# Expert feed-forward stage of a graph layer: node tiles in groups of four instead of two

## What is computed

```python
def _L0_ffn_ref(x, Wr, br, W1, b1, g1, be1, m1, v1, W2, b2, g2, be2, m2, v2, Wo, bo):
    feat = jnp.mean(x, axis=0)
    w = jax.nn.softmax(feat @ Wr + br, axis=-1)
    h = jnp.einsum('bfd,edh->bfeh', x, W1) + b1
    h = jax.nn.relu(_bn(h, g1, be1, m1, v1))
    h = jnp.einsum('bfeh,ehk->bfek', h, W2) + b2
    h = jax.nn.relu(_bn(h, g2, be2, m2, v2))
    y = jnp.einsum('bfeh,ehd->bfed', h, Wo) + bo
    return jnp.einsum('bfed,fe->bfd', y, w)
...
x = x + _L0_ffn_ref(_layernorm(x, axis=-1)[None], ...)[0]
```

## Time and profile before

| | |
|---|---|
| runs | 2795.51, 2791.87, 2793.63 us; median 2793.63 |
| span of the profiled execution | 2870.7 us |
| PE busy in it | 2525.6 us, 88% |
| DVE, ACT, POOL busy | 2235.1, 1570.5, 930.4 us |
| chain that ended last, by engine | PE 67%, DVE 19%, issue 7% |
| chain that ended last, L1378 and L1388 | 20% and 10% |

### The profile page before, as it was taken

One profiled execution on the slowest core, in us unless ns is written; L12 is line 12 of the kernel. 1 busy time (PEld: TensorE's weight loads), 2 busy tenths in 40 slices (PEclk: granted clock), 3 DMA queues, 4 the chain that ended last, 5 costly groups with the idle time before them and its releaser, 6 DMA issues.

```text
span 2870.7 us, 48875 instructions
## 1 busy us (share of the span) xinstructions
PE 2525.6 (88%) x15682; PEld 2185.1 (76%) x15682; DVE 2235.1 (78%) x4426; ACT 1570.5 (55%) x3233; POOL 930.4 (32%) x891
## 2 busy tenths in 40 slices
PE   6379995788988889988888989858999999999999
PEld 4266773567767767767767767648999999999999
DVE  6796553698998899899898899857777777777775
ACT  5422110355555656556555555546666666666665
POOL 0140003456666666656666666600000000000000
PEclk9798997799999999999999999978999999999999
DMA  5031445566666666666666666630000000000000
GB/s 157 22 108 43 139 137 178 147 192 190 194 195 192 193 196 194 189 193 192 198 197 190 189 194 194 189 100 12 16 16 16 12 14 14 16 16 16 16 14 10
DMA packets 190069, 336.68 MB, mean 117 GB/s; under 512 B 31472, under 2 KB 129040, under 8 KB 189798
## 3 DMA queue, kind: packets, MB, share of 16 engines
q0 software_dynamic: 67104, 219.09, 25.4%
q1 hardware_dynamic: 122726, 114.53, 13.2%
HBM read 293.83 MB, written 40.48 MB: 116 GB/s over the span
## 4 chain that ended last, share of the span: by engine, by line
PE 67%; DVE 19%; issue 7%; another core or an unknown queue 2%; ACT 1%; DMA 1%; DVEq 1%; SPq 0%; POOL 0%; ACTq 0%; POOLq 0%
PE ps L1378 20%; PE ps L1274 10%; PE ps L1388 10%; PE ps L1263 7%; PE ps L1140 4%; DVE ring L1726 3%; PE ps L1241 3%; PE ps L1234 3%; DVE ring L1779 2%; DVE rows L1478 2%; PE ps L1219 1%; PE ps L1056 1%; DVE nodes L1793 1%; PE ps L1063 1%
## 5 line engine op out<-in xcount | busy, mean ns | idle before, releaser
L798 POOL DMA_INDIRECT ring<-kv_rows,idx x832 | 877.2, 1054 | 796.5 <-DMA idx<-src_cols 276.3
L1378 PE MATMUL ps<-f_split,e_up 128*128 128x256 f32 (+1 forms) x3200 | 595.4, 287 | 5.0 <-DVE e_low L1938 5.0
L980 ACT ACTIVATE f_more<-ps,e_rest 128x256 f32<-128x256 f32 (+1 forms) x800 | 401.9, 552 | 259.5 <-PE ps L1378 257.4
L1378 PEld LDWEIGHTS ps<-f_split,e_up 128*128 128x128 f32 x3200 | 501.0, 193 | 9.3 <-DVE e_low L1938 5.7
L1263 PE MATMUL ps<-nodes,ohT 128*128 x1664 | 418.1, 396 | 89.2 <-issue 62.6
L1274 PE MATMUL ps<-ring 128*128 128x260 f32 x1664 | 454.5, 420 | 0.0
L1378 PE MATMUL ps<-f_split,e_low 128*128 128x256 f32 (+1 forms) x1600 | 454.3, 284 | 0.0
L1263 PEld LDWEIGHTS ps<-nodes,ohT 128*128 128x128 f32 x1664 | 321.4, 198 | 163.1 <-issue 116.1
L1914 DVE TENSOR_TENSOR f_split<-f_more,f_split 128x512 fp32r<-128x512 f32 (+1 forms) x400 | 272.6, 681 | 200.9 <-ACT f_split L985 194.0
L1274 PEld LDWEIGHTS ps<-ring 128*128 128x128 f32 x1664 | 322.7, 204 | 45.7
L912 ACT ACTIVATE nodes<-ps 128x780 f32 x208 | 170.8, 821 | 297.6 <-PE ps L1274 250.2
(11 more groups left out here) (341 smaller groups left out, 3626.0 us busy)
## 6 DMA issues: line engine op xcount, KB each, us to landing
relq<-rel_rows SPq DMA_DIRECT2D x208, 128.0 KB
ring<-kv_rows,idx POOLq DMA_INDIRECT x832
kv_rows<-work SPq DMA_DIRECT2D x49, 256.0 KB, 2.1
xn_rows<-nodes SPq DMA_DIRECT2D x1, 6272.0 KB, 22.1
sx_rows<-work SPq DMA_DIRECT2D x49, 128.0 KB, 1.8
nodes<-in_x_dram SPq DMA_DIRECT2D x4, 1536.0 KB
work<-in_x_dram SPq DMA_DIRECT2D x48, 128.0 KB, 2.1
m_xn<-xn_rows SPq DMA_DIRECT2D x24, 256.0 KB
```

What stands on the lines that cost most here:

```text
L798: pool.indirect_dma_start(out=kvh(c)[:, g, 0:2 * D], out_offset=None, in_=kvD, in_offset=bass.IndirectOffsetOnAxis(ap=idx[c // KP][:, s:s ...
L980: ins = act.activation(f_whole[l][:, m * T2 * P:m * T2 * P + n * P], bank(2 * l + e % 2, m * T2 * P, m * T2 * P + n * P), ACT.Relu, bias=e ...
L1378: last = pe.matmul(bank(2 * l + e % 2, m * T2 * P, m * T2 * P + n * P), e_parts[l][w][:, e, i, m * P:(m + 1) * P], src_[a][:, i * T2 * P:i ...
```

## The change

Groups now have up to four tiles (`T4`): 3, ten times 4, 3 and 3 tiles (`FGROUPS`), 13 groups instead of 25. Layers 0 and 1 stream 512 columns (384 in groups of three) past each weight block. A half of such a layer fills a whole PSUM bank, so each layer takes banks 2l and 2l + 1 and the last layer banks 4 and 5, with no second buffer: `f_h`, the PSUM results and the waits are for one unit (`reuse(u, 1)`). The sum is made in place in `nodes` (L1862 wrote `f_y` before), SP's store reads it there, and `y_stored` is gone; the layer norm's output shares the buffer `f_res` with the residual rows that SP loads. At the start of the stage layer 0 of unit 1 comes later on each engine. Unit order on PE is otherwise the same.

```diff
-    NG2 = (NW - 1) // T2
-    WT = T2 * D
+    T4 = 4
+    FGROUPS = [3] + [T4] * ((NW - 9) // T4) + [3, 3]
+    NFG = len(FGROUPS)
+    FSTART = [sum(FGROUPS[:g]) for g in range(NFG)]
+    assert sum(FGROUPS) == NW
+    WT = T4 * D
     NG = (NW - 1) // TG
...
         f_whole = [cut(f_more, WT * l, WT) for l in range(2)]
-        f_y = [cut(f_more, WT * (2 + b), WT) for b in range(2)]
-        f_z, f_zT = [cut(f_zz, WT * i, WT) for i in range(2)]
-        f_res = [cut(f_res2, WT * b, WT) for b in range(2)]
+        f_z = f_res
 
         def spread(t, n):
...
-        f_rc = cut(small, 96, T2 * H)
-        f_m = cut(small, 112, T2)
-        f_st, f_mv, f_rs = m_st, m_mv, m_rs
+            return t[:, :] if n == T4 else t.rearrange("p (m a) -> p m a", m=NF)[:, :, 0:n * P]
+
+        def nodes_of(g, n):
+
+            return nodes[:, FSTART[g] * AC:(FSTART[g] + n) * AC].rearrange("p (t a) -> p t a", a=AC)
...
+            def out_store(g):
+                n = FGROUPS[g] - (g == NFG - 1)
+                y = nodes_of(g, FGROUPS[g])
                 sp.wait_ge(sem("y_made"), done(g * NE + (NE - 1)))
-                if n == T2:
-                    sp.dma_start(tiles2(out, g, n), f_y[b].rearrange("p (t d) -> p t d", d=D)).then_inc(sem("out_sent"), 16)
-                else:
-                    sp.dma_start(out[(NW - 1) * P:N, :], f_y[b][0:TAIL, 0:D]).then_inc(sem("out_sent"), 16)
-                sp.wait_ge(sem("out_sent"), g * 16 + 16)
-                sp.sem_inc(sem("y_stored"), 1)
-            sp.sem_inc(sem("y_stored"), CREDIT)
...
+            res_load(0)
+            sp.wait_ge(sem("f_T_ps"), done(0))
+            res_load(1)
+            for g in range(NFG):
+                if g + 2 < NFG:
+                    sp.wait_ge(sem("f_T_ps"), done(g + 1))
+                    res_load(g + 2)
+                out_store(g)
...
             def layer(l, u, e, n):
 
-                s_ps, s_sb, s_lo, s_next = (("l1_ps", "h1_sb", "h1_lo", "l2_ps"), ("l2_ps", "h2_sb", "h2_lo", "l3_ps"))[l]
+                s_ps, s_sb, s_lo = (("l1_ps", "h1_sb", "h1_lo"), ("l2_ps", "h2_sb", "h2_lo"))[l]
                 act.wait_ge(sem(s_ps), done(u))
                 act.wait_ge(sem(s_lo), reuse(u, 1))
-                act.wait_ge(sem(s_next), reuse(u, 2))
                 for m in range(NF):
-                    ins = act.activation(f_whole[l][:, m * T2 * P:m * T2 * P + n * P], bank(2 * l + e % 2, m * T2 * P, m * T2 * P + n * P), ACT.Relu,
+                    ins = act.activation(f_whole[l][:, m * QW:m * QW + n * P], bank(2 * l + m, 0, n * P), ACT.Relu,
                                          bias=e_sh[l][:, e * NF + m:e * NF + m + 1], scale=e_sc[l][:, e * NF + m:e * NF + m + 1])
                 ins.then_inc(sem(s_sb), 1)
                 if l == 0:
                     act.wait_ge(sem(s_sb), done(u))
-                    act.activation(spread(f_h[l][e % 2][0], n), spread(f_whole[l], n), ACT.Copy).then_inc(sem("h1_up"), 1)
+                    act.wait_ge(sem("l2_ps"), reuse(u, 1))
+                    act.activation(spread(f_h[l][0], n), spread(f_whole[l], n), ACT.Copy).then_inc(sem("h1_up"), 1)
...
-            layer(0, 0, 0, T2)
-            layer(0, 1, 1, T2)
+                first_part(0, 0, F0, q)
+            layer(0, 0, 0, F0)
             for q in range(6, NE):
-                first_part(0, 0, T2, q)
+                first_part(0, 0, F0, q)
             upper(2)
-            layer(1, 0, 0, T2)
...
+            layer(0, 1, 1, F0)
+            layer(1, 0, 0, F0)
+            for g, n in enumerate(FGROUPS):
+                experts(g, g % 2, n, FGROUPS[g + 1] if g + 1 < NFG else 0)
...
-                s_ps, s_sb, src_ = (("l1_ps", "h1_sb", f_T[b]), ("l2_ps", "h2_sb", f_h[0][e % 2]))[l]
+                s_ps, s_sb, src_ = (("l1_ps", "h1_sb", f_T[b]), ("l2_ps", "h2_sb", f_h[0]))[l]
                 if l == 1:
                     pe.wait_ge(sem("h1_lo"), done(u))
                 elif e == 0:
                     pe.wait_ge(sem("f_T_lo"), done(g))
-                pe.wait_ge(sem(s_sb), reuse(u, 2))
+                pe.wait_ge(sem(s_sb), reuse(u, 1))
                 for m in range(NF):
                     for i in range(NF):
                         for w, a in PASSES:
-                            last = pe.matmul(bank(2 * l + e % 2, m * T2 * P, m * T2 * P + n * P), e_parts[l][w][:, e, i, m * P:(m + 1) * P],
-                                             src_[a][:, i * T2 * P:i * T2 * P + n * P], start=(i == 0 and w + a == 0), stop=(i == NF - 1 and w == 1))
+                            last = pe.matmul(bank(2 * l + m, 0, n * P), e_parts[l][w][:, e, i, m * P:(m + 1) * P],
+                                             src_[a][:, i * QW:i * QW + n * P], start=(i == 0 and w + a == 0), stop=(i == NF - 1 and w == 1))
                 last.then_inc(sem(s_ps), 1)
...
-                pe.wait_ge(sem("y_made"), reuse(u, 2))
+                pe.wait_ge(sem("y_made"), reuse(u, 1))
                 for t in range(n):
                     for i in range(NF):
                         for w, a in PASSES:
-                            last = pe.matmul(bank(4 + e % 2, t * D, (t + 1) * D), f_h[1][e % 2][a][:, i * T2 * P + t * P:i * T2 * P + (t + 1) * P],
+                            last = pe.matmul(ps[:, 4 * 512 + t * D:4 * 512 + (t + 1) * D], f_h[1][a][:, i * QW + t * P:i * QW + (t + 1) * P],
...
-            layer(0, 0, 0, 0, 0, T2)
-            layer(0, 1, 1, 0, 0, T2)
+            layer(0, 0, 0, 0, 0, F0)
             for q in range(5, NE):
-                first_part(0, 0, T2, q)
+                first_part(0, 0, F0, q)
+            layer(0, 1, 1, 0, 0, F0)
             pe.wait_ge(sem("e_ready"), 4)
-            layer(1, 0, 0, 0, 0, T2)
+            layer(1, 0, 0, 0, 0, F0)
             pe.wait_ge(sem("e_ready"), 5)
...
-                y = f_y[b]
-                av = nodes[:, ds(g * (T2 * AC), n * AC)].rearrange("p (t a) -> p t a", a=AC)
...
+                av = nodes_of(g, n)
+                y = av[:, :, 0:D]
...
-                    dve.wait_ge(sem("y_stored"), reuse(g, 2))
...
+                    y4 = y.rearrange("p t (h c) -> p t h c", h=H)
+                    go(dve.tensor_tensor(y4, y4,
...
-                    dve.wait_ge(sem(f"res_in{b}"), m * 16 + 16)
-                    go(dve.tensor_tensor(y[:, 0:n * D], y[:, 0:n * D], f_res[b][:, 0:n * D], ALU.add))
+                    dve.wait_ge(sem("res_in"), g * 16 + 16)
+                    go(dve.tensor_tensor(y, y, rows_of(f_res), ALU.add))
...
             def lower(l, u, e, n):
 
-                up, lo = [spread(t, n) for t in f_h[l][e % 2]]
+                up, lo = [spread(t, n) for t in f_h[l]]
                 whole = spread(f_whole[l], n)
                 if l == 0:
                     dve.wait_ge(sem("h1_up"), done(u))
                 else:
                     dve.wait_ge(sem("h2_sb"), done(u))
+                    dve.wait_ge(sem("l3_ps"), reuse(u, 1))
                     dve.tensor_copy(up, whole).then_inc(sem("h2_up"), 1)
                     dve.wait_ge(sem("h2_up"), done(u))
                 dve.tensor_tensor(lo, whole, up.bitcast(F32), ALU.subtract).then_inc(sem(("h1_lo", "h2_lo")[l]), 1)
...
-                        yt = f_y[b][:, t * D:(t + 1) * D]
-                        ins = dve.scalar_tensor_tensor(out=yt, in0=bank(4 + e % 2, t * D, (t + 1) * D), scalar=f_w[b][:, t * NE + e:t * NE + e + 1],
+                        yt = nodes_of(g, n)[:, t, 0:D]
+                        ins = dve.scalar_tensor_tensor(out=yt, in0=ps[:, 4 * 512 + t * D:4 * 512 + (t + 1) * D], scalar=f_w[b][:, t * NE + e:t * NE + e + 1],
...
-            lower(0, 0, 0, T2)
+            lower(0, 0, 0, F0)
             weights_low(1)
-            lower(0, 1, 1, T2)
             for q in range(6, NE):
-                first_part(0, 0, 0, T2, q, go)
+                first_part(0, 0, F0, q, go)
+            lower(0, 1, 1, F0)
             weights_low(2)
-            lower(1, 0, 0, T2)
```

126 lines of the change are left out of this document (53 added, 73 removed).

## The result

The changed kernel takes 2760.8 us (median of four, 2756.1 to 2767.0) beside 2792.8 for the kernel before (four, 2790.4 to 2795.5): a ratio of 0.9893, 95% interval 0.9875 to 0.9911, or about 30 us less. A second series on one chip gave 2761.2 against 2792.3, 0.9885 (0.9867 to 0.9904).

A forecast was written before the change was run, and what follows sets the result against it. PE's matmul streaming at full clock was taken to bound the feed-forward stage. Its terms summed to 878.8 against 905.8 us (-27.0); start +8.7 and end +1.3 left -17.0, so 2793.6 became 2777 us, range 2764 to 2790.

The forecast's parts named there:

- its own signs: Trace checks: wrong if wide matmuls are 0.24 or under 0.225 apart, PE idles before last layers, or the edge stage moves.
- Wider matmuls: Layers 0 and 1 on PE: 512 columns cost 0.2333 us against 0.240 for two of 256; layers 832.0 against 856.6.
- the interpolation to 384: Groups of three on PE: 384 columns cost 0.1767 us, estimated on the line between 256 and 512 columns.
- Rival B: PE's weight load was the limit and 512 columns run at 0.2133 to 0.2267: 2739 to 2764 us; chance 0.10.
- First parts: Each group's first part on PE: 0.93 us a tile plus 0.27 fixed, 45.8 us in all against 50.0.
- Does the single buffer hold: Timetable of a four-tile unit: no PE stall, slack 2.0 us ordinarily, 0.9 with piece 0; about 1.0 us in all.
- Rival D: The last layer's single buffer stalls PE in every unit, 0.5 us beyond the slack: 2829 us; chance 0.05.
- the second half of C: DVE's piece 0 stalls PE in each group, +13 us: 2790; chance 0.16 shared with 512 columns costing 0.240.
- The end: Last layers of units 6 and 7 wait 0.9 and 2.9 us, 3.8 against 0.9; sums and stores after add 1.3.
- The start: Third tile and new DVE order delay the third low weights, done at 1968.4 instead of 1959.7: +8.7 us.
- this slow turn: First 24 matmuls behind the third low weights run at the low clock: 2.6 us extra.
- Carrying the difference over: The profiled span's -17.0 us applied to the median, 2793.6 to 2777, though that span is 77 us over it.

The follow-up runs named there:

- e1_halves: Changed kernel with layers 0 and 1 in groups of four streamed as two halves of 256 columns per weight block; 0.9975 of the kernel before, stage 933.4 us.
- e9_forms: Changed kernel plus blocks of 48 matmuls behind its last sum, other engines silent, varying form, bank, weights, stream and width; every 512-column form took 0.2267 us a matmul.
- e3_twos: Changed kernel's code with groups of two tiles and a last one of one tile; 1.0061 of the kernel before, stage 963.0 us.
- e5_start: Changed kernel with VectorE making the third low weights ahead of unit 1's first low parts; 0.9870 of the kernel before, stage 904.8 us.
- e7_start: Repeat, beside the changed kernel on one chip, of its edit making the third low weights ahead of unit 1's low parts; 2756.8 us, 0.9871 of the kernel before.

## Why the prediction was wrong

By its own signs the mechanism stands: wide matmuls are neither at 0.24 nor under 0.225, PE doesn't idle ahead of the last layer in mid-stage, and the chain is the one described. (That the edge stage ended 85 us earlier says nothing; it is the same program and differs between executions.) What failed is the size of one term.

From the third low weights to PE's end the prediction had 878.8 us; the trace has 2749.79 - 1881.76 = 868.0. The start is 6.9 longer, not 8.7, the tail behind the last matmul 1.8, not 1.3. Together -38.2 + 6.9 + 1.8 = -29.5, where the sum had -17.0.

- **Wider matmuls: the step that failed, by its size.** The mechanism is right (e1_halves: the width of the groups of four alone is 22.4 us, where the prediction had 12.8), but in this stage 512 columns cost 0.228 and not 0.2333. That is 1920 x (0.2333 - 0.2279) = 10.4 us, which is why a group takes 70.7 and not 71.8, and the three groups of three add 576 x (0.1767 - 0.1733) = 2.0. These 12.4, less the 1.15 that the clock took back at the end, are the 10.8 between 878.8 and 868.0, to half a microsecond. The error was to carry a price over from another stage, where 5 ns of it decide the sum. The row was of the same form, operand type and clock, and it took thirty matmuls in a row; still its 0.2333 holds 6.6 ns that alone the same form doesn't show (e9_forms). Against a price of 0.240 for two halves that surplus halves the gain. I had the earlier trace rows to warn me: 128 columns at 0.1117 and 256 at 0.120, which is 256/2.4 + 13.3 ns. The same 13.3 ns above the columns gives 0.1733 for 384 and 0.2267 for 512, what the runs measured; and the interpolation to 384 leaned on the wrong end point too.
- **Rival B had the number, and its reason is neither shown nor refuted.** 0.2267 was its upper end, and its 2764 was nearest to the result. In e9_forms one and the same block throughout costs the same 10.88 us as a new one each time, but the trace has 48 weight loads for those 48 matmuls too, so this run doesn't take the load away. 448, 320 and 192 columns cost about 0.203, 0.147 and 0.111. Down to 256 columns all prices are the columns' time plus about 13 ns (448 is nearer 16); 192 and 128 sit on a floor of 0.111. So two halves pay the 13.3 ns twice and a whole pays it once: that is the 0.2400 - 0.2267. Whether the load or the matmul costs them stays open. The Trainium skill, page "TensorE: Matmul & The Clock Gate", section "Back-to-back issue gap", has N/2.4 + 2.5 ns for the gap of isolated matmuls (the prediction used it for a stream), 216 ns at 512 columns, and about 131 ns at 512 for a sustained stream of loads and matmuls. The rows agree with neither: they have 227 ns, 13.3 in the place of 2.5, and by the page's 2.5 the change would have gained 2.5 ns a pair (an estimate from its figure) and not 12.
- **First parts: right.** 70.69 - 8 x 8.34 = 4.0 us for a group of four, as forecast.
- **Does the single buffer hold: right, and closer than worked out.** PE doesn't wait for it in mid-stage. The ordinary unit has 1.5 us of room and not 2.0, the unit with piece 0 has 0.4 and not 0.9. Rival D and the second half of C were rightly small, but C's was 0.4 us away. At groups of two the same buffer costs 20 us (e3_twos), which the prediction never asked about, since it went straight to four.
- **The end: right in its waits, short by a clock.** The turns of unit 6 and 7 wait 0.9 and 2.9 as forecast (2741.09 and 2746.45, each 2.97 behind the turn ahead of it; in the first of them PE still had 12 matmuls). But the last turn takes 3.31 us where the turn before the waits took 2.16, because the granted clock fell inside it. The windows of after (columns as in the earlier trace rows):

```profile
2743.50:2746.40 2.90, 0.00 (x0) 0.00 (x0) 2.70 (x5) 0.00 (x0) 0.00 (x0) 1.00 0.00 0
2746.50:2748.00 1.50, 1.50 (x11) 1.50 (x12) 0.00 (x0) 0.00 (x0) 0.00 (x0) 0.85 0.00 0
2748.00:2749.70 1.70, 1.70 (x9) 1.46 (x7) 0.00 (x0) 0.00 (x0) 0.00 (x0) 0.50 0.00 0
```

  PE stood idle for 3 us at clock 1.00, began again at 1.00, and ran the second half of the turn at 0.50 (1.2 GHz). So the stretch of the 3 us wait and the turn behind it cost 4 us more than the turn alone would at 1.00.
- **The start: right in kind.** The new order is what makes it longer, as the bracket of 3.02 us shows; I had it 1.8 us too long. e5_start and e7_start take 4.0 of the 6.9 back, and the stage gains 6.2 to 6.4, since the turn behind no longer meets the half clock. The prediction had this slow turn at 2.6 us above its price at the full clock, as before the change; it was 2.8.
- **Carrying the difference over** from a profiled execution 77 us above the median to the median was sound: the stage's difference, 29.5, is that of the times, 31.9 and 31.1, within their spread.
